# A threshold search and its choice moved between steps of an attention loop on VectorE

## The reference

```python
q = (hidden_states @ q_proj_w.T).reshape(B, Q, NUM_HEADS, HEAD_DIM).transpose(0, 2, 1, 3)
k = (cross_attention_states @ k_proj_w.T).reshape(B, KV, NUM_KV_HEADS, HEAD_DIM).transpose(0, 2, 1, 3)
v = (cross_attention_states @ v_proj_w.T).reshape(B, KV, NUM_KV_HEADS, HEAD_DIM).transpose(0, 2, 1, 3)
q, k = rmsnorm(q, q_norm_w), rmsnorm(jnp.repeat(k, n_rep, axis=1), k_norm_w)
attn = jax.nn.softmax(jnp.einsum('bhqd,bhkd->bhqk', q, k) * scale + attention_mask, axis=-1)
out = jnp.einsum('bhqk,bhkd->bhqd', attn, v).transpose(0, 2, 1, 3).reshape(B, Q, -1) @ o_proj_w.T
```

```python
_, topk_idx = jax.lax.top_k(cm, k)
mask = jnp.zeros((B, L, C), x.dtype).at[b_idx, l_idx, topk_idx].set(1.0)
crucial_features = mask_moved * x
subcrucial_features = (1.0 - mask_moved) * x
```

## Time and profile before

| what | value |
|---|---|
| time, three runs | 864.17, 867.71, 871.29 us (median 867.71) |
| profiled execution | 866.43 us |
| its span | 864.3 us |
| TensorE busy | 779.7 us, 90% of the span |
| VectorE busy | 715.1 us, 83% |
| ScalarE busy | 522.2 us, 60% |
| GpSimd busy | 415.8 us, 48% |
| granted TensorE clock, mean | 0.974 of 2.4 GHz |

### The profile page before, as it was taken

One profiled execution on the slowest core, in us unless ns is written; L12 is line 12 of the kernel. 1 busy time (PEld: TensorE's weight loads), 2 busy tenths in 40 slices (PEclk: granted clock), 3 DMA queues, 4 the chain that ended last, 5 costly groups with the idle time before them and its releaser, 6 DMA issues. The chain is left out here.

```text
span 864.3 us, 16319 instructions
## 1 busy us (share of the span) xinstructions
PE 779.7 (90%) x5146; PEld 631.4 (73%) x5146; DVE 715.1 (83%) x1743; ACT 522.2 (60%) x1414; POOL 415.8 (48%) x372
## 2 busy tenths in 40 slices
PE   1976799858988999999999999999999999788878
PEld 0475577534677898898898888888888888675446
DVE  7877998969787887887897897897897897787975
ACT  6875798745556657557557657657657556551521
POOL 3237068715036745845744845745746645511110
PEclk9998999979999999999999999999999999899989
DMA  8255236544020310310220220320220220003001
GB/s 300 101 164 155 73 123 229 173 126 149 26 74 21 119 35 20 97 54 3 94 73 0 97 73 0 97 73 0 97 73 0 74 75 1 26 1 119 0 1 49
DMA packets 37775, 66.20 MB, mean 77 GB/s; under 512 B 5537, under 2 KB 17889, under 8 KB 37602
## 3 DMA queue, kind: packets, MB, share of 16 engines
q1 hardware_dynamic: 37730, 65.63, 23.2%
HBM read 60.28 MB, written 5.34 MB: 76 GB/s over the span
## 5 line engine op out<-in xcount | busy, mean ns | idle before, releaser
L2377 DVE TENSOR_SCALAR_CACHE_REDUCE xn<-ctxT,candidate 128x512 bf16<-128x512 f32 x240 | 168.8, 741 | 0.0
L2029 ACT ACTIVATE layer_attention_probs<-xnT,stats 128x512 f32<-128x512 f32 x128 | 93.9, 734 | 123.2 <-DVE stats L2172 123.2
L1764 PE MATMUL bank<-layer_attention_keysT,layer_attention_queriesT 128*128 128x512 f32 x384 | 121.9, 426 | 5.0 <-DVE layer_attention_queriesT L2165 5.0
L2184 DVE TENSOR_TENSOR layer_attention_probsT<-bank,layer_attention_probsT 128x512 fp32r<-128x512 f32 x128 | 88.1, 688 | 44.7 <-ACT layer_attention_probsT L2037 43.2
L1764 PEld LDWEIGHTS bank<-layer_attention_probsT,layer_attention_values 128*128 128x128 f32 x768 | 99.6, 190 | 13.4 <-DVE layer_attention_probsT L2184 6.0
L1764 PE MATMUL bank<-layer_attention_probsT,layer_attention_values 128*128 128x256 f32 x768 | 102.4, 283 | 5.1 <-DVE layer_attention_probsT L2184 5.1
L2037 ACT CAST layer_attention_probsT<-bank 128x512 fp32r<-128x512 f32 x128 | 74.9, 585 | 52.3 <-PE bank L1840 48.4
L1764 PE MATMUL bank<-layer_attention_l_wq,layer_attention_xnT 128*128 128x512 f32 x384 | 93.5, 392 | 0.0
L1764 PEld LDWEIGHTS bank<-layer_attention_l_wkv,layer_context_parts 128*128 128x128 f32 x720 | 88.5, 188 | 2.8
L1764 PE MATMUL bank<-layer_attention_l_wkv,layer_context_parts 128*128 128x256 f32 x720 | 90.5, 278 | 0.0
L1764 PE MATMUL bank<-layer_attention_wo,layer_attention_headsT 128*128 128x512 f32 x336 | 88.8, 406 | 0.0
(11 more groups left out here) (338 smaller groups left out, 1717.7 us busy)
## 6 DMA issues: line engine op xcount, KB each, us to landing
layer_attention_l_raw_qo<-in_wqT SPq DMA_DIRECT2D x8, 1024.0 KB, 5.5
layer_attention_l_raw_qo<-in_woT SPq DMA_DIRECT2D x8, 1024.0 KB, 6.5
xnT<-inverse_sums SPq DMA_DIRECT2D x15, 512.0 KB, 3.8
tw_raw<-in_w_gateT SPq DMA_DIRECT2D x8, 688.0 KB, 5.2
tw_raw<-in_w_upT SPq DMA_DIRECT2D x8, 688.0 KB, 4.3
tw_raw<-in_w_downT SPq DMA_DIRECT2D x6, 768.0 KB, 4.7
layer_attention_l_raw_kv<-in_wkvT SPq DMA_DIRECT2D x8, 512.0 KB, 4.8
ternary<-tw_rounded SPq DMA_DIRECT2D x8, 344.0 KB, 2.5
```

What stands on the lines that cost most here:

```text
L1764: last = pe.matmul(out, stationary[f][a], moving[f][b], start=f == 0 and x == 0, stop=f == count - 1 and x == 2)
L2029: a.activation(probs[:, u % 3, :], masked[:, u % 2, :], ACT.Exp, bias=negmax[:, u:u + 1], scale=-1.0, accum_out=sums[:, u:u + 1]).then_inc ...
L2184: v.tensor_tensor(probsT[:, 1, p % 2, :, columns], T[u % 2][:, :].rearrange("p (c q) -> p c q", c=CPB), probsT[:, 0, p % 2, :, columns], A ...
L2377: own(k.nc.vector.tensor_scalar((k.flags if flags is None else flags)[:, r % 2], row_tile(k.ctxT, r), k.candidate[:, r:r + 1].bitcast(F32) ...
```

## The change

On VectorE the loop makes five passes instead of six. Each pass has five rounds in its two steps instead of four: units 3 and 7 have two pairs of counts, the others one (`COUNTS`), and an update follows every fourth pair wherever that falls. In the odd step these are units 3 (between its two pairs) and 6, in the even step units 1, 4 and 7 (behind its second pair). Steps 11 to 14 are written out behind the loop. Step 11 has two rounds as before; steps 12, 13, 14 and 15 have one choice each (0, 2, 4, 6). In steps 12 to 14 the pieces stand in units 1, 3, 4, 6 and 7, in the final step in units 0 to 4. The tail has no choice any more. The number of rounds stays the same: before, 28 in steps 0 to 13 and one in step 14; after, two in step 0, 25 in the loop and two in step 11. The other engines keep their six passes and their order; the values that VectorE waits for on `bisection` are worked out anew.

```diff
-    CHOICE = {STEPS - 2: (0,), STEPS - 1: (2, 4)}
+    CHOICE = {STEPS - 4: (0,), STEPS - 3: (2,), STEPS - 2: (4,), STEPS - 1: (6,)}
     LOOPED = STEPS // 2 - 2
-    FINAL_PIECES = (1, 1, 1, 1, 1, 1, 1, 1)
+    SEARCHED = 5
+    COUNTS = (1, 1, 1, 2, 1, 1, 1, 2)
+    FINAL_PIECES = (1, 1, 1, 1, 1, 0, 0, 0)
     OWN_START, OWN_STEP = BISECT_PER_ROUND - 2 * FRONT_COUNTS, 2 * BISECT_PER_ROUND
-    OWN_AT = {x: OWN_START + OWN_STEP * x for x in (0, 1, 2, STEPS - 3, STEPS - 2)}
-    OWN_AT[STEPS - 1] = OWN_AT[STEPS - 2] + BISECT_PER_ROUND + CHOICE_COUNT
-    OWN_END = OWN_AT[STEPS - 1] + 2 * CHOICE_COUNT
+    OWN_PAIR = 5 * BISECT_PER_ROUND
+    OWN_AT = {0: OWN_START, 1: OWN_START + OWN_STEP}
+    OWN_AT[2] = OWN_AT[1] + 2 * sum(COUNTS) + 2 * 5
+    OWN_AT[STEPS - 5] = OWN_AT[1] + SEARCHED * OWN_PAIR
+    OWN_AT[STEPS - 4] = OWN_AT[STEPS - 5] + OWN_STEP
+    for x in range(STEPS - 3, STEPS):
+        OWN_AT[x] = OWN_AT[x - 1] + CHOICE_COUNT
+    OWN_END = OWN_AT[STEPS - 1] + CHOICE_COUNT
...
-                    chosen_from = UNITS - 4 if pairs else UNITS
+                    counts = COUNTS if step[0] is not None else (1,) * UNITS
+                    counted = sum(COUNTS) if step[0] is not None and step[1] == 2 else 0
...
-                        if u < chosen_from:
-                            bisection_count(k, own, u % 4)
-                            if u % 4 == 3:
-                                bisection_update(k, own)
+                        if not pairs:
+                            for j in range(counted, counted + counts[u]):
+                                bisection_count(k, own, j % 4)
+                                if j % 4 == 3:
+                                    bisection_update(k, own)
+                            counted += counts[u]
                         else:
-                            units = UNITS - chosen_from
-                            at_u = [(x - chosen_from) * len(pieces) // units for x in (u, u + 1)]
+                            at_u = [x * len(pieces) // UNITS for x in (u, u + 1)]
                             for r, piece in pieces[at_u[0]:at_u[1]]:
                                 choose_piece(k, own, r, piece)
...
-                with v.Fori(0, LOOPED) as i:
+                with v.Fori(0, SEARCHED) as i:
                     run((i, 1))
                     run((i, 2))
-                run((None, STEPS - 3))
+                for step in range(2 * SEARCHED + 1, STEPS - 2):
+                    run((None, step))
                 run((None, STEPS - 2))
                 run_final()
...
-                k.flags = gated[:, 0, 0, :, :].rearrange("p b c -> p (b c)").bitcast(BF16).rearrange("p (j c) -> p j c", j=2)
-                for piece in range(CHOICE_PIECES):
-                    choose_piece(k, own, CTILES - 2, piece)
```

More of the change, by code:

```diff
@@ L2202, in run_final @@
                     before = after(final, -1)
-                    own = LoopOwn(v, S_["bisection"], None, 2 * OWN_STEP, OWN_AT[STEPS - 1])
+                    own = LoopOwn(v, S_["bisection"], None, OWN_PAIR, OWN_AT[STEPS - 1])
                     pieces = [(r, piece) for r in CHOICE[STEPS - 1] for piece in range(CHOICE_PIECES)]
@@ L2233, in run @@
                     following, before = after(step), after(step, -1)
-                    own = LoopOwn(v, S_["bisection"], step[0], 2 * OWN_STEP, OWN_AT[step[1]])
+                    own = LoopOwn(v, S_["bisection"], step[0], OWN_PAIR, OWN_AT[step[1]])
                     pairs = CHOICE.get(step[1], ())
                     pieces = [(r, piece) for r in pairs for piece in range(CHOICE_PIECES)]
-                    chosen_from = UNITS - 4 if pairs else UNITS
+                    counts = COUNTS if step[0] is not None else (1,) * UNITS
+                    counted = sum(COUNTS) if step[0] is not None and step[1] == 2 else 0
                     for u in range(UNITS):
@@ L2290, in _ @@
                  .then_inc(S_["keyscale_ready"], 1)
-                own = LoopOwn(v, S_["bisection"], None, 2 * OWN_STEP, 0)
+                own = LoopOwn(v, S_["bisection"], None, OWN_PAIR, 0)
                 values_low(start, 0)
```

## The result

The changed kernel takes 884.06 us (median of four runs, 883.21 to 888.09), the kernel before 865.94 beside it: a ratio of 1.0225, interval 1.0189 to 1.0262. The profiled execution took 883.21 us, with a span of 881.5 against 864.3. In the changed kernel's file lines move by 7 (L1709 is L1716, L1764 is L1771, L2184 is L2191) or, behind the search's edits, by 10 (L2427 is L2437); in VectorE's tail, which lost a choice, it is 7 again (L2653 is L2660).

What follows compares the result with a forecast made beforehand. TensorE sets the pace, while VectorE seems to have 4 to 6 us spare a step. Terms 6.0 + 2.0 + 9.7 - 0.7 - 1.9 - 0.6 = +14.5 us on 866.4 give 881 us, range 866 to 892.

Steps and rivals of the forecast that it cites:

- 69.7 forecast: Sign of being right: windows of two loop steps near 69.7 us, where they are 65.9 now.
- Part 1: Loop's odd steps: later maximum, scores and unit 7 cost 1.2 us a pair of steps, +6.0 (2 to 7.5).
- Part 2: Even steps, units 1 to 6: updates not wholly covered by VectorE's idle time, +2.0 us (0 to 5).
- Part 3: End of each even step: second pair lengthens VectorE's chain and the update meets GpSimd's L1709, +9.7 us (+2.4 to +11).
- third rival: Slower still: new waits of 2.2 us lower TensorE's clock in the loop, 2.3 us each, five times: 893 us; chance 0.14.
- A clock of 0.5 inside the loop: Sign of being wrong: the granted clock at 0.5, the 1.2 GHz level, inside the loop.
- Part 4: Steps 11 to 14: end of step 12 gives -0.7 us, step 14's single last piece -1.9 (0 to -4.2).
- the forecast's 3.0: TensorE's wait ahead of the final step, 4.93 us before, would be near 3 us.
- Part 5: Final step gives 0; in the tail the logits' addition comes earlier until TensorE is late, -0.6 us (-0.4 to -0.7).
- the longer list of stalls: Rule holding for GpSimd's power L1696 too: updates in even units 4 lose about 1 us more, up to 5 in all.

Runs made afterwards that it cites:

- loop_alone: Changed kernel's loop of five rounds in two steps, but the choices stand where the kernel before has them; 883.5 us, ratio 1.0206.
- even7_moved: Changed kernel with the second pair of counts of even steps' unit 7 moved to unit 2; 876.46 us, ratio 1.0137.
- even14: Changed kernel with the two second pairs of an even step in units 1 and 4, updates in units 1, 4 and 7; 875.54 us, ratio 1.0117.
- odd8: Changed kernel with all four additional pairs of a pass in even steps' units 1, 4, 5 and 6; 864.24 us, ratio 0.9983.
- odd3_moved: Changed kernel with the second pair of odd steps' unit 3 moved to unit 2, and the update with it; 905.76 us, ratio 1.0474.
- ends_alone: Loop counts of the kernel before, choices where the change puts them, five search rounds left out; 862.73 us, ratio 0.9981.
- three_pairs: Changed kernel with three pairs of counts and no update in even steps' unit 7; 875.8 us, ratio 1.0115.
- pieces_early: Changed kernel with the five pieces of a choice in units 0 to 4 of steps 12, 13 and 14; 878.1 us, ratio 1.0127.

## Why the prediction was right

**The mechanism.** Forecast 881 us, measured 884.06. The dearest place was the end of the even steps, for the reason given: the added pair moves the update from a place ahead of GpSimd's product into it. The runs show the parts: the pair alone makes 1.0 us of wait (loop_alone, its last pass), the meeting lifts that to between 2.15 and 2.47, and without a second pair there (even7_moved, even14, odd8) nothing is lost at 14 ends of 15; the one that lost 1.5 met the product with its single pair. Two loop steps take 69.6 us where the clock stays up, for the 69.7 forecast, and 71.1 where it falls.

**Part 1** (odd steps, 1.2 a pair of steps) measures 1.37 in the pass of the table: 0.64 at unit 5 for 0.45, 0.34 for the 0.6 at the scores, 0.39 behind the end for 0.15. Together 6.9 for +6.0. That the held update by itself costs nothing is shown by odd8, as by the kernel before.

**Part 2** (middle of the even steps, +2.0) was too high: these windows did not grow. It was no free place, though: even7_moved and even14 lose 1.67 and 1.5 there with other orders.

**Part 3** (+9.7). 2.30 to 2.47 of wait for the 2.2 above 0.16 that I had taken. All of the loop is +22.0, less 6.9 for part 1 leaves 15.1 where 9.7 stood. The missing 5 us are the third rival, which came in part: behind three of the five waits the clock fell, and TensorE's busy time in those windows (steps 5, 7 and 11) is 35.71, 35.77 and 34.45 us, against 34.14 and 34.18 in the two of the loop that did not and 32.83 in step 11 before, 1.6 each, not the 2.3 that I had priced. A clock of 0.5 inside the loop was also one of the prediction's own signs of being wrong, and for the clock it holds: the forecast's sum had no such term in the loop.

**Part 4.** Step 13's window gave 1.4 for the -0.7. From step 14 to 15 the wait fell by 0.73, not 1.9: in this execution this step of the argument failed. I took the last piece alone to wait for one GpSimd instruction; it waited for the product behind that too, by the timelines of GpSimd and VectorE, from 762.79 to 766.82. That was the term's own upper end ("0, if L1709 gets ahead of it"). It is a race: of the seven traces with the choices in these places, four have a wait of 4.18 to 4.20 us (the changed kernel, odd3_moved, even14, odd8) and three one of 2.87 or 2.88 (ends_alone, even7_moved, three_pairs), a fall of 2.05 and near the forecast's 3.0. pieces_early shows that the piece was the cause of the wait.

**Part 5.** -0.6 in the tail is as read: the addition waits 4.47 us for TensorE. The final step gave nothing by itself.

**Sums.** Loop +22.0 for +17.7, ends -4.2 for -3.2. The loop's excess is the clock; the range to 892 held it because the third rival was in it. That the total came within 3 us is in part luck: part 2's 2.0 did not come while the clock's 4.8 did, and of the ends' -4.2, 1.4 lies behind the logits' addition, with one low stretch of the clock fewer, which no part of the sum named and ends_alone does not have.

**The rule and the rows.** Nothing here speaks for the longer list of stalls that I set aside: in the changed kernel's odd step 9 the update's last instructions (579.60 to 580.09) run at 0.16 to 0.20 us each beside GpSimd's power (579.59 to 580.60). The Trainium skill, "SBUF — State Buffer", section "SBUF: two separate sides", lets a VectorE instruction with two SBUF inputs wait for the whole of a GpSimd instruction that reads SBUF. The products and the lower halves of weights agree: 1.60 beside 1.59 us, 2.20 beside 2.36; the power again does not.

## What to carry to other kernels

An engine's idle sum says that work fits, not where: the fifth round's four pairs in a pass cost 22.0 us from step 0's reciprocal to step 11's in one place and 3.0 in another (odd8: 366.31 against 363.31). Before moving an instruction, lay its new time beside what the neighbour engine runs then, and once more after the delay that the move itself makes; in odd3_moved, and in the final step of pieces_early, the new neighbour was one that the old trace did not show there. A short instruction that waits matters by what is queued behind it: the update held for 2.28 us in odd unit 3 was free as long as no second pair stood behind it.

## What the runs showed of the hardware

- The clock did not fall by the length of the wait alone. Behind waits of 2.43, 2.38 and 2.35 us the granted clock was 0.64, 0.65 and 0.61 over the next 4.4 to 4.8 us, so for most of it at the lower level of 1.2 GHz; behind 2.30 and 2.47 us, in the same kernel and at the same place of other passes, it stayed at 1.00. In pieces_early the clock fell behind a wait of 2.38 us at the end of step 8 and not behind one of 2.38 at the end of step 10; in loop_alone it fell behind 2.20 and not behind 2.26. What tells them apart is open. Two of the windows, of the changed kernel:

```profile
421.75:426.51 4.76, 4.76 (x27) 4.76 (x28) 4.51 (x13) 2.47 (x6) 3.22 (x4) 0.64 0.19 71
564.06:566.50 2.44, 2.44 (x21) 2.44 (x22) 2.34 (x7) 1.56 (x4) 1.64 (x3) 1.00 0.25 95
```

- An instruction with one tensor input is held as well. The comparison L2414 (128x256, two of them) took 1.35 to 2.73 us at its four places in pieces_early, beside GpSimd's L1722 or the product, and 0.60 to 0.61 at its four places in the changed kernel; the shift of the bits (L2442, 128x16) took 1.55 at the end of step 4 and 0.17 at that of step 8. The counts (L2387), which have one tensor input too, took 0.73 to 0.75 at all 248 places in the changed kernel, beside GpSimd's work as well.
